# A four-layer graph network on one core: distinct nodes in empty lanes, the fourth layer's map turned a batch ahead, and edge values moved behind a scan

## The reference

```python
x = ln(x + segment_sum(h[dst], src))                  # 1: h = x W^T + b
x = ln(x + relu(ln(mlp(x + segment_sum(x[src], dst)) + x)))          # 2
x = ln(x + bn_relu(bn_relu(x + segment_sum(w * x[dst], src))))      # 3
h = lrelu(x @ w_W + w_b);  edge_h = lrelu(edge_attr @ ew_W + ew_b)   # 4
e = concat([h[src], h[dst], edge_h]) @ a_W + a_b
alpha = softmax of e over the edges of one src
x = ln(x + lrelu(segment_sum(alpha * h[dst], src)))
```

## Time and profile before

| | us |
|---|---|
| median of 3 runs | 5461.24 (5458.34 to 5461.74) |
| the profiled execution's own time | 5449.37 |
| its span | 5447.6 |
| POOL busy | 3880.5 (71%) |
| DVE busy | 3616.6 (66%) |
| PE busy | 3119.4 (57%) |
| ACT busy | 1572.9 (29%) |
| first gather of layer 4 | 4332.19 |
| last gather of layer 4 starts | 5390.10 |

### The profile page before, as it was taken

One profiled execution on the slowest core, in us unless ns is written; L12 is line 12 of the kernel. 1 busy time (PEld: TensorE's weight loads), 2 busy tenths in 40 slices (PEclk: granted clock), 3 DMA queues, 4 the chain that ended last, 5 costly groups with the idle time before them and its releaser, 6 DMA issues. The chain is left out here.

```text
span 5447.6 us, 60777 instructions
## 1 busy us (share of the span) xinstructions
PE 3119.4 (57%) x13489; PEld 2467.7 (45%) x13489; DVE 3616.6 (66%) x11648; ACT 1572.9 (29%) x4853; POOL 3880.5 (71%) x4057
## 2 busy tenths in 40 slices
PE   5777776233433333555455465665666577767765
PEld 3555554133333333444444344444443455555554
DVE  9999998455555555666666555555555567777776
ACT  3222222000000000000000122222225367777775
POOL 6777777777777776777777577777771177777774
PEclk9999898566555655766766678778777788888888
DMA  4222222077777776777777533333331233433434
GB/s 109 74 76 76 76 77 73 13 214 221 224 220 225 221 221 192 215 215 214 216 215 215 159 105 105 105 105 105 105 105 31 66 105 108 112 110 110 112 110 73
DMA packets 307824, 740.57 MB, mean 136 GB/s; under 512 B 88393, under 2 KB 116253, under 8 KB 307491
## 3 DMA queue, kind: packets, MB, share of 16 engines
q0 software_dynamic: 230160, 629.44, 40.9%
q1 hardware_dynamic: 77331, 107.50, 6.5%
HBM read 689.24 MB, written 47.41 MB: 135 GB/s over the span
## 5 line engine op out<-in xcount | busy, mean ns | idle before, releaser
L2007 DVE TENSOR_TENSOR ACC<-ps,ACC 128x256 f32 x2352 | 998.2, 424 | 778.2 <-PE ps L1378 507.3
L782 POOL DMA_INDIRECT ZT<-table,meta_dst x832 | 805.7, 968 | 437.7 <-issue 189.8
L1378 PE MATMUL ps<-ZT_parts,xT_parts 128*128 128x256 f32 x3136 | 701.0, 410 | 517.9 <-DMA ZT_parts<-table,meta_src 272.7
L715 POOL DMA_INDIRECT rec_src<-ZT x800 | 775.1, 969 | 261.1 <-issue 238.4
L782 POOL DMA_INDIRECT ZT<-table,meta_src x784 | 743.3, 948 | 276.5 <-issue 159.0
L782 POOL DMA_INDIRECT ZT_parts<-table,meta_dst x784 | 746.6, 952 | 252.5 <-issue 165.4
L1378 PEld LDWEIGHTS ps<-ZT_parts,xT_parts 128*128 128x128 f32 x3136 | 668.1, 320 | 547.2 <-DMA ZT_parts<-table,meta_src 285.6
L782 POOL DMA_INDIRECT ZT_parts<-table,meta_src x784 | 745.6, 951 | 238.9 <-issue 160.9
L1405 PE MATMUL ps<-ZT,xT 128*128 128x256 f32 x1664 | 520.7, 458 | 197.2 <-DVE X L2322 178.9
L1378 PE MATMUL ps<-ZT,xT 128*128 128x256 f32 x1568 | 511.0, 497 | 139.4 <-DMA ZT<-table,meta_src 139.4
L1378 PEld LDWEIGHTS ps<-ZT,xT 128*128 128x128 f32 x1568 | 404.3, 261 | 248.4 <-DMA ZT<-table,meta_src 159.1
(11 more groups left out here) (447 smaller groups left out, 5533.5 us busy)
## 6 DMA issues: line engine op xcount, KB each, us to landing
ACC<-in_edge_attr SPq DMA_DIRECT2D x200, 240.0 KB
ZT<-table,meta_dst POOLq DMA_INDIRECT x832
rec_src<-ZT POOLq DMA_INDIRECT x800
ZT_parts<-table,meta_src POOLq DMA_INDIRECT x784
ZT_parts<-table,meta_dst POOLq DMA_INDIRECT x784
ZT<-table,meta_src POOLq DMA_INDIRECT x784
table<-meta_dst SPq DMA_DIRECT2D x24, 512.0 KB
table<-meta_dst SPq DMA_DIRECT2D x47, 256.0 KB
```

The lines of the kernel that those rows point to most:

```text
L715: pool.indirect_dma_start(rec_src, bass.IndirectOffsetOnAxis(ap=rec_of[0][:, c:c + 1], axis=0), pay_src[:, c, :], None).then_inc(scattered ...
L782: pool.indirect_dma_start(slot(s), None, rows, bass.IndirectOffsetOnAxis(ap=ids[:, s, 0:1].bitcast(I32), axis=0)).then_inc(gathered[s // G ...
L1378: mm = nc.tensor.matmul(o, chosen, part, start=(i == 0), stop=(i == len(parts) - 1))
L2007: v.tensor_tensor(dst, slot_sum(j), dst, ALU.add).then_inc(sem["added"], 1)
```

## The change

Three edits. The pads' field 0 gets 9 times the lane's running number in place of zero, so that empty lanes name distinct nodes. The turn of batch b + 1 of the fourth layer's map is issued by PE ahead of the rows of batch b, and the first batch's turn ahead of the loop and of the wait for the split bias. `edge_values` of group g + 3 goes from behind the fourth sum of group g to behind its scan.

```diff
+PAD_STEP = 9
@@ PE, map of the fourth layer
-            def node_rows(b, q, nt):
+            def node_columns(b, q, nt):
                 wait(pe, sem["rows_done"], b + (ROWS[2] + 1))
                 turn(3, acc3)(b, q, nt)
+
+            def node_rows(b, q, nt):
+                if b + 1 < NB:
+                    node_columns(b + 1, 1 - q, min(SB, T - (b + 1) * SB))
                 wait(pe, sem["xT_sbuf"], b * 2 + (XS[3] + 2))
                 rows_out(b, nt, lambda k, j: xT[:, q, k, j * P:(j + 1) * P], 0, 4 + 2 * q, YB[3] - 1, bias16[:, 0, :])
+            node_columns(0, 0, SB)
             pe.wait_ge(sem["split_ready"], 3)
             each_batch(node_rows)
@@ DVE, start
+            dve.wait_ge(sem["consts"], 6)
+            link(v.tensor_scalar(mv[:, 0, 0:1], lane_no[:, :], 5.0 * PAD_STEP, None, ALU.mult))
             for rec in (meta_src, meta_dst):
                 link(v.memset(rec[:, 0:5, :], 0.0))
-                v.memset(rec[:, 0:5, 1], NO_EDGE).then_inc(sem["zeroed"], 1)
+                link(v.memset(rec[:, 0:5, 1], NO_EDGE))
+                v.tensor_scalar(rec[:, 0:5, 0], iota[:, 0:5], float(PAD_STEP), mv[:, 0, 0:1], ALU.mult, ALU.add).then_inc(sem["zeroed"], 1)
             v.memset(attr[96:P, :, :, :], 0.0).then_inc(sem["zeroed"], 1)
             link(v.memset(zsum[:, :, :, :], 0.0))
-            dve.wait_ge(sem["consts"], 6)
@@ DVE, attend
                         maxima(*after(i, k, 2), j - 2)
-                    if j == 3 and (not last or k + 3 < RG):
-                        edge_values(*after(i, k, 3), *ring_group_3(b, u, k + 3))
                 wait(dve, sem["run_done"], g)
                 dve.wait_ge(sem["probT_ready"], g * G + G)
                 c = bass.ds(i * R + (k * G + 1), G)
                 v.tensor_tensor_scan(wsum[:, c], corr[:, q, :], rsum[:, q, :], wsum[:, bass.ds(i * R + k * G, 1)],
                                      ALU.mult, ALU.add).then_inc(sem["run_done"], 1)
+                if not last or k + 3 < RG:
+                    edge_values(*after(i, k, 3), *ring_group_3(b, u, k + 3))
```

More of the change, by code:

```diff
@@ L54 @@
 NO_EDGE = -100000.0
+PAD_STEP = 9
+assert PAD_STEP * (5 * P - 1) < N_NODES
 UC = 7
```

## The result

The changed kernel takes 5484.68 us (median of 6 runs, 5480.41 to 5488.58) and the kernel before, beside it, 5458.86 (5455.23 to 5461.74): a ratio of 1.0049, 95% interval 1.0039 to 1.0059. The forecast was 5487. The profiled execution took 5481.52 us with a span of 5479.8, against 5449.37 and 5447.6.

What follows compares the result with a forecast made beforehand. POOL's gathers were taken to pace layer 4, at 40.74 us a round. Start +0.6, map -15, third edit with tail +40 made +26 us: 5475 for the profiled execution, 5487 as median, range 5436 to 5517.

Steps and rivals of the forecast that it cites:

- Edit 2: Fourth layer's map: turning ahead hides ACT's copy, batch 6.19 to 4.95 or 4.8 us; 15 us less, bounds 13 and 17.
- Edit 1, start: Kernel start: DVE's wait for constants and three small operations for the pads add 0.6 us, between 0 and 1.
- Edit 1, landings: Fourth layer's last groups: distinct rows land every 10.18 us, not 14.0; group 103 readable 11.6 us earlier, bounds 0 and 12.
- Edit 3, the size: Fourth layer: DVE waits on the chain through ACT and PE; round 43.0 us against POOL's 40.74, last group read 54 late.
- Edit 3, the share of slow turns: PE's turns of logits in layer 4: nine in ten at 1.2 GHz after standing, adding 2.2 us a round over POOL's pace.
- rival C: Layer 4: slow clock takes in slot sums, ACT's table change delays turns; up to 1.5 us a round more, 5520; chance 0.15.
- Rival A: Layer 4: clock holds, turns quick, round stays at POOL's 40.74 us; 28 us less, 5433; chance 0.19.
- The tail: After layer 4's last read: four sums and the scan already done, PE's turn not behind delayed slot sums; 2 us less.
- The sum: Whole kernel: +0.6 - 15 + 40 = +26 us on the profiled execution's 5449.4, giving 5475; 5487 as median.

Runs made afterwards that it cites:

- e_12_again: Changed kernel with its third edit taken back (edge values at the fourth sum), run again, against the kernel before: 5419.91 us against 5447.14, ratio 0.9946.
- e_12: Changed kernel with its third edit taken back (edge values at the fourth sum), against the kernel before: 6474.87 us against 6484.79, ratio 0.9986.

## Why the prediction was right, and where its steps were not

- **Edit 2.** Batch 4.95 or 4.8 forecast, 4.77 measured; first gather near 4317 forecast, 4317.46 in e_12_again and 4319.94 after the change (the two run the same code up to there, so 2.5 us is what executions and chips differ by). Right.
- **Edit 1, start.** +0.6 forecast. DVE's first reduction over the node numbers starts at 8.96 in place of 7.99: +0.97, as one of the three small operations took 0.49. Whether this 1 us reaches layer 4 can't be told from 2.5 us of spread.
- **Edit 1, landings.** 10.18 us a group forecast, 10.2 measured without edit 3; DMA share 0.39. Swallowed in the changed kernel, as forecast: no read of pads waits for its landing. Right.
- **Edit 3, the size.** Round 43.0 forecast, 43.10 measured; last group read 54 us behind the ordinary landing forecast. With 57.6 between the two traces' stages (e_12_again has the ordinary landings) the term was 4 short. Position 1, with the finished rows' work, took 11.32 for 11.28. Right in size, and right that the chain comparisons, mask, turn, maximum is where DVE stands, 170 us in all; what stretches that chain is the next two points.
- **Edit 3, the share of slow turns.** This step was wrong. "I let nine turns in ten be slow": 18 of 86 lasted over 1.7 us (13 + 4 + 1), 25 over 1.2. "PE stands 3.5 us ahead of every turn" holds for two positions of four; in 1 and 3 other work of PE stands directly ahead and the turn is quick. The row of 1.97 us that the prediction gives to the group ahead is the first half of the same group's slot sums (4464.83 and 4469.35); the change of level across the stand is as it says.
- **What made up for it.** Position 3, for which I took 10.66 us slow and 9.73 quick, took 11.36 with a quick turn. What rival C described, at a chance of 0.15, happens: the turn stands behind slot sums that ACT's table change delays, in every round from group 19 on, and the low clock takes in these slot sums in 13 of 21. The price of 33 us that C put on top of the forecast isn't there, as the slow turns that it was added to are few. From the rows: quick throughout would be 9.8 (positions 0 and 2, as groups 38 and 40: 9.75 and 9.80) + 11.3 + 9.8 + 10.8 (group 39) = 41.7 us; the other 1.4 us is the low level of the clock, 0.55 in position 0, 0.3 in position 2 and 0.55 in position 3, where it is the slot sums' (5.70 for 4.25). This split is worked out from rows; no run where POOL sets the pace tried it. Against the prediction's 40.5 (3 x 9.73 + 11.28) I had left out 1.1 us of position 3, and I had put 2.8 x 0.9 = 2.5 us on the clock. That 43.0 met 43.10 is luck: 1.1 us too little in one term and 1.1 too much in the other.
- **Rival A** ("quick, the stage still fits", 5433) counted on a round of 40.5. With quick turns it would have been some 41.7, by this count, and the kernel about (41.7 - 40.74) x 25 = 24 us behind its 5433. That is worked out, not measured.
- **The tail.** -2 forecast, -0.3 measured.
- **The sum.** +26 forecast for the profiled execution, +32.2 measured; +25.8 between the medians. The profiled execution before lay 11.9 us under the median of its three runs, the one after 3.2 under the median of its six, so that 5487 comes within 3 us of the median is luck in part.

By the rule that the prediction took from the Trainium skill (TensorE: Matmul & The Clock Gate, "HAM oscillation — how this bites in real kernels"), that short bursts behind longer waits lose the full clock in every pass, every turn would have been slow. The traces agree in part: the stage's granted clock fell from 0.88 to 0.79 with the stands, and is 0.88 without edit 3. But after the same 3.2 us of standing a turn took 1.97 us at 4723.87 and 1.09 at 4766.34: the stand ahead of a burst doesn't say by itself at which of the two levels, 1.2 or 2.4 GHz, it runs. What told it in position 0 was the level of the slot sums of position 3, in 21 rounds of 21; in position 2 it stays open.

## What to carry to other kernels

Before moving a step to behind a barrier, follow what it feeds through all engines back to the engine itself, for each position of the round separately: extra jobs cover the wait in one position and lengthen it in another. A round's length can come out right with the wrong parts, so check a forecast at its parts. The version to keep here is the change without its third edit (e_12_again, 5420 us against 5447): DVE stands 76.9 us in all for landings there, and the stage is still 57.6 us shorter, as sums 5 to 8 and the scan lie beside the chain.

## What the runs showed of the hardware

**128 lanes that name one row.** An indirect gather of 128 equal rows keeps the DMA engines at 0.82 for 81 GB/s, and its group of eight lands every 14.0 us; with distinct rows the same slots go at 0.39 and 106 GB/s, every 10.2 us (e_12_again).

**Chips on which the same kernel is slower.** e_12 and e_12_again are one kernel: 6474.87 and 5419.91 us. The longest waits of e_12:

```profile
PEld ps L1380 <- issue: 1407.0, 682, 23.7
DVE ACC L2016 <- remote: 793.2, 181, 9.6
...
ACT ends L929 <- issue: 762.7, 34, 38.5
```

In e_12_again PE's largest such wait in total is this one, and no stand at all is put down to "remote":

```profile
PEld ps L1407 <- issue: 199.8, 118, 5.8
```

"issue" is time in which the engine waited for nothing that the profile shows. The two instruction queues carried the same 110 and 223 packets in both. It looks as if PE's instructions came late, by up to 23.7 us, and engines that wait for PE's signals with them; the traces don't show the cause. Five of the six comparisons behind the result's fell on such chips, numbers 3, 4, 5 (twice) and 15; e_12_again, on number 9, ran between them, so it isn't the hour alone. What makes a chip so isn't shown.
